# Rotation of K on GpSimd from a ScalarE copy, that of Q left on VectorE, and x2 plus its norm as one affine step of ScalarE

## What is computed

```python
x = x + L0_attn(layernorm(x))                      # stage A
u = layernorm(x)                                   # stage B from here
q = xpos(u @ Wq, inverse_scale=False)              # x * cos + rot * sin
k = xpos(ctx_1024 @ Wk, inverse_scale=True)
v = ctx_1024 @ Wv
x = x + (q @ k^T * decay_mask) @ v                 # x2
y = layernorm(x)
x = x + (y + moe_top2(rms_norm(y)))                # 8 experts, the FFN has its own skip
```

## Time and profile before

| | us |
|---|---|
| median of 3 runs | 457.16 (456.96 to 457.54) |
| the profiled execution, its own time | 458.88 |
| its span, first to last instruction | 457.1 |
| PE, DVE, ACT, POOL busy | 380.0, 275.5, 258.8, 199.6 |
| granted TensorE clock, mean | 0.931 of full |

### The profile page before, as it was taken

The page is one execution under the profiler, slowest core; times in us unless marked ns, Lnnn a source line. Parts: engine busy times, 40 slices in busy tenths (PEclk is TensorE's granted clock), DMA queues, the critical chain, the costliest instruction groups (busy, mean ns, idle before and its releaser), DMA issues.

```text
span 457.1 us, 10128 instructions
## 1 busy us (share of the span) xinstructions
PE 380.0 (83%) x2600; PEld 272.5 (60%) x2601; DVE 275.5 (60%) x688; ACT 258.8 (57%) x473; POOL 199.6 (44%) x186
## 2 busy tenths in 40 slices
PE   1899997899885211499999999999999999999980
PEld 0687786787774211256666666666666666666650
DVE  3789787979797999554444444454444444444440
ACT  2799786776775631555445545554555555554530
POOL 2634637668788403224343334343443344333221
PEclk9999998999998555599999999999999999999996
DMA  7999850622221240112222222222222322223220
GB/s 248 408 426 403 288 184 1 204 73 70 69 93 62 77 142 1 36 29 45 48 36 36 45 47 35 44 39 47 43 37 37 47 47 35 36 45 45 26 25 11
DMA packets 24645, 41.93 MB, mean 92 GB/s; under 512 B 5040, under 2 KB 20400, under 8 KB 23600
## 3 DMA queue, kind: packets, MB, share of 16 engines
q1 hardware_dynamic: 17088, 31.17, 19.1%
q0 software_dynamic: 7536, 10.52, 14.3%
HBM read 32.17 MB, written 9.50 MB: 91 GB/s over the span
## 4 chain that ended last, share of the span: by engine, by line
PE 67%; DVE 13%; ACT 8%; issue 5%; POOL 2%; DMA 2%; SPq 1%; ACTq 0%; DVEq 0%; POOLq 0%
PE bank L1220 30%; PE bank L1241 6%; PE bank L1270 5%; PE bank L1271 5%; PE bank L1272 5%; ACT arena L434 4%; DVE expert_w L842 3%; PE bank L1107 2%; PE bank L1155 2%; PE bank L1252 2%; DVE expert_w L833 2%; ACT arena L449 2%; PE bank L1164 2%; PE bank L1060 1%; DVE arena L988 1%
## 5 line engine op out<-in xcount | busy, mean ns | idle before, releaser
L1220 PE MATMUL bank<-expert_w,arena 128*128 x702 | 159.2, 364 | 4.4 <-ACT arena L617 4.4
L732 POOL DMA_INDIRECT out<-arena,add_idx x39 | 61.7, 1581 | 114.8 <-ACT arena L598 114.8
L1220 PEld LDWEIGHTS bank<-expert_w,arena 128*128 128x128 f16 x702 | 65.8, 98 | 54.2 <-issue 6.8
L1037 DVE SCALAR_TENSOR_TENSOR arena<-bank,dn_small,arena 128x512 f32<-128x512 f32 x78 | 45.3, 581 | 38.2 <-PE bank L1220 23.4
L722 POOL DMA_INDIRECT arena<-xrow_hbm,take_idx x39 | 38.7, 994 | 58.1 <-PE bank L1252 43.3
L1270 PE MATMUL bank<-expert_w,arena 128*128 x195 | 53.1, 273 | 0.9 <-DVE arena L1021 0.9
L1271 PE MATMUL bank<-expert_w,arena 128*128 x195 | 53.2, 273 | 0.0
L1272 PE MATMUL bank<-expert_w,arena 128*128 x195 | 53.1, 273 | 0.0
L1021 DVE COPY arena<-bank 128x1024 f16<-128x1024 f16 x39 | 27.0, 692 | 37.8 <-PE bank L1241 37.8
L617 ACT ACTIVATE arena<-bank 128x512 f16<-128x512 f16 x39 | 23.3, 597 | 37.1 <-PE bank L1252 37.1
L1043 DVE TENSOR_TENSOR arena<-arena 128x512 f16<-128x512 f32 x39 | 27.0, 692 | 27.1 <-ACT arena L623 27.1
(11 more groups left out here) (179 smaller groups left out, 736.5 us busy)
## 6 DMA issues: line engine op xcount, KB each, us to landing
expert_w<-in_wup SPq DMA_DIRECT2D x8, 1408.0 KB, 17.2
expert_w<-in_wdn SPq DMA_DIRECT2D x10, 640.0 KB, 4.7
rows<-in_x SPq DMA_DIRECT2D x8, 256.0 KB, 6.3
arena<-in_ctxT SPq DMA_DIRECT2D x8, 256.0 KB, 3.2
xrow_hbm<-front SPq DMA_DIRECT2D x8, 256.0 KB, 2.2
out<-rows SPq DMA_DIRECT2D x8, 256.0 KB, 2.7
expert_w<-in_wdn SPq DMA_DIRECT2D x20, 64.0 KB, 4.9
cst_b<-in_consts_b SPq DMA_DIRECT2D x1, 960.0 KB, 13.6
```

The lines of the kernel that those rows point to most:

```text
L732: pool.indirect_dma_start(out=out, in_=yt[:, i % 2], in_offset=None, out_offset=bass.IndirectOffsetOnAxis(ap=add_idx[:, i:i + 1], axis=0), ...
L1037: V.scalar_tensor_tensor(out=hh[:, cols], in0=src, scalar=h_scale[:, ds(e, 1)], in1=sg[:, cols], op0=ALU.mult, op1=ALU.mult).then_inc(s_h, 1)
L1220: last = T.matmul(bank[q][:, 0:n], xsT[:, slot, (2 * a + c) * P:(2 * a + c + 1) * P], up_w[:, ds(w0 + c * UPC + w * 2 * H + lo, n)], start ...
```

## The change

On the K half, ScalarE copies PSUM bank 2 into the SBUF tile `kc` (it takes the place of `sk`) as soon as K is ready. GpSimd then does everything from that copy: the cosine product, the two sine products, a wait for its own products (`s_krot`), and the addition. VectorE keeps the products of Q only, and the addition for Q stays on GpSimd, now behind the four instructions for K.

For x2 plus its norm, GpSimd adds 1 to the reciprocal root, and ScalarE computes row * (1 + r) + bias in place in one pair of instructions, late in its step, behind the transposed copy and the high part of xn. The ScalarE pair in front of u2 and the GpSimd addition L690 are gone.

```diff
 # ScalarE, step_b
-                if live(r, 3, NBATCH):
-                    act.wait_ge(s_r34, b + 1)
-                    if r >= 4:
-                        act.wait_ge(s_x2s, b)
-                    for j in range(2):
-                        last = nc.scalar.activation(sk[:, j], rows[:, ds(b * 2 + j, 1), :].squeeze(1), ACT.Identity,
-                                                    bias=nb3[:, slot, j:j + 1], scale=r34[:, slot, 0, j:j + 1])
-                    last.then_inc(s_s, 1)
...
                 if live(r, 1, NBATCH):
                     b, _, slot = at(it, k, 1)
+                    act.wait_ge(s_K, b + 1)
+                    if r >= 2:
+                        act.wait_ge(s_kr, b)
+                    nc.scalar.activation(kc, bank[2][:, :].rearrange("p (m n) -> p m n", m=2), ACT.Copy).then_inc(s_rk, 1)
                     act.wait_ge(s_V, b + 1)
...
                     if r < NBATCH + 2:
                         xn_high(b)
+                    act.wait_ge(s_r34, b + 1)
+                    act.wait_ge(s_xn, b + 1)
+                    for j in range(2):
+                        row = rows[:, ds(b * 2 + j, 1), :].squeeze(1)
+                        last = nc.scalar.activation(row, row, ACT.Identity, bias=nb3[:, slot, j:j + 1],
+                                                    scale=ve3[:, slot, 0, j:j + 1])
+                    last.then_inc(s_x2s, 1)
 # GpSimd, step_b
-                    for n, (bank_read, rotated, dst) in enumerate(((s_rk, s_kr, kr), (s_rq, s_qr, qr))):
-                        pool.wait_ge(bank_read, b + 1)
-                        if n and r >= 3:
-                            pool.wait_ge(s_xn, b - 1)
-                        nc.gpsimd.tensor_tensor(dst[:, slot], dst[:, slot], rot[:, n], ALU.add).then_inc(rotated, 1)
+                    pool.wait_ge(s_rk, b + 1)
...
+                    nc.gpsimd.tensor_tensor(kr[:, slot], kc, const("kcos").unsqueeze(1).broadcast_to([P, 2, SEQ]), ALU.mult)
+                    for m in range(2):
+                        last = nc.gpsimd.tensor_tensor(rot[:, 0, m], kc[:, 1 - m], const("ksin")[:, m * SEQ:(m + 1) * SEQ], ALU.mult)
+                    last.then_inc(s_krot, 1)
+                    pool.wait_ge(s_krot, b + 1)
+                    nc.gpsimd.tensor_tensor(kr[:, slot], kr[:, slot], rot[:, 0], ALU.add).then_inc(s_kr, 1)
+                    pool.wait_ge(s_rq, b + 1)
+                    if r >= 3:
+                        pool.wait_ge(s_xn, b - 1)
+                    nc.gpsimd.tensor_tensor(qr[:, slot], qr[:, slot], rot[:, 1], ALU.add).then_inc(s_qr, 1)
...
-                    pool.wait_ge(s_s, b + 1)
-                    pool.wait_ge(s_xn, b + 1)
-                    nc.gpsimd.tensor_tensor(rows[:, ds(b * 2, 2), :], sk, rows[:, ds(b * 2, 2), :], ALU.add).then_inc(s_x2s, 1)
...
+                    nc.gpsimd.tensor_tensor(ve3[:, slot, 0], r34[:, slot, 0], const("ones")[:, 0:2], ALU.add)
 # VectorE, step_b
-                    for n, (ready, rotated, read, used, dst, cos, sin) in enumerate((
-                            (s_K, s_kr, s_rk, s_R, kr, const("kcos"), const("ksin")),
-                            (s_Q, s_qr, s_rq, s_R, qr, const("qcos"), const("qsin")))):
...
+                    V.tensor_tensor(qr[:, slot], src, const("qcos").unsqueeze(1).broadcast_to([P, 2, SEQ]), ALU.mult)
+                    for m in range(2):
+                        last = V.tensor_tensor(rot[:, 1, m], src[:, 1 - m], const("qsin")[:, m * SEQ:(m + 1) * SEQ], ALU.mult)
+                    last.then_inc(s_rq, 1)
```

More of the change, by code:

```diff
@@ L177, in build @@
         xn = view(arena, 4480, 2, D)
-        sk = view(arena, 4992, 2, D)
+        kc = view(arena, 4992, 2, SEQ)
         xnT = view(arena, 5504, 2, SEQ)
@@ L255, in build @@
         s_rk, s_rq = sem("k_bank_read"), sem("q_bank_read")
-        s_kr, s_qr = sem("k_rotated"), sem("q_rotated")
+        s_kr, s_qr, s_krot = sem("k_rotated"), sem("q_rotated"), sem("k_products_ready")
         s_vt = sem("v_copied")
@@ L261, in build @@
         s_pp = sem("pool_step")
-        s_s, s_x2s, s_out0 = sem("skip_ready"), sem("x2_plus_skip_ready"), sem("skip_stored")
+        s_x2s, s_out0 = sem("x2_plus_skip_ready"), sem("skip_stored")
         s_xh, s_xl, s_xn = sem("xn_high_ready"), sem("xn_low_ready"), sem("xn_ready")
@@ L554, in step_b @@
                 if live(r, 3, NBATCH):
-                    b, _, _ = at(it, k, 3)
+                    b, _, slot = at(it, k, 3)
                     act.wait_ge(s_tr3, b + 1)
@@ L679, in step_b @@
                     b, _, slot = at(it, k, 1)
[L680 to L684 removed]
+                    pool.wait_ge(s_rk, b + 1)
+                    if r == 1:
+                        pool.wait_ge(s_cstb, 16)
+                    if r >= 3:
+                        pool.wait_ge(s_R, b - 1)
+                    if r >= 2:
+                        pool.wait_ge(s_kr, b)
+                    nc.gpsimd.tensor_tensor(kr[:, slot], kc, const("kcos").unsqueeze(1).broadcast_to([P, 2, SEQ]), ALU.mult)
[5 more added lines that the diff above has]
+                    pool.wait_ge(s_rq, b + 1)
+                    if r >= 3:
+                        pool.wait_ge(s_xn, b - 1)
+                    nc.gpsimd.tensor_tensor(qr[:, slot], qr[:, slot], rot[:, 1], ALU.add).then_inc(s_qr, 1)
                 if live(r, 3, NBATCH):
                     b, _, _ = at(it, k, 3)
[L688 to L690 removed]
                     pool.wait_ge(s_xh, b + 1)
@@ L858, in step_b @@
                     b, _, slot = at(it, k, 1)
-                    for n, (ready, rotated, read, used, dst, cos, sin) in enumerate((
-                            (s_K, s_kr, s_rk, s_R, kr, const("kcos"), const("ksin")),
-                            (s_Q, s_qr, s_rq, s_R, qr, const("qcos"), const("qsin")))):
-                        src = bank[2 + n][:, :].rearrange("p (m n) -> p m n", m=2)
-                        dve.wait_ge(ready, b + 1)
-                        if r >= 2:
-                            dve.wait_ge(rotated, b)
-                        if r >= 3:
-                            dve.wait_ge(used, b - 1)
-                        V.tensor_tensor(dst[:, slot], src, cos.unsqueeze(1).broadcast_to([P, 2, SEQ]), ALU.mult)
-                        for m in range(2):
-                            last = V.tensor_tensor(rot[:, n, m], src[:, 1 - m], sin[:, m * SEQ:(m + 1) * SEQ], ALU.mult)
-                        last.then_inc(read, 1)
+                    src = bank[3][:, :].rearrange("p (m n) -> p m n", m=2)
+                    dve.wait_ge(s_Q, b + 1)
+                    if r >= 2:
+                        dve.wait_ge(s_qr, b)
+                    if r >= 3:
+                        dve.wait_ge(s_R, b - 1)
+                    V.tensor_tensor(qr[:, slot], src, const("qcos").unsqueeze(1).broadcast_to([P, 2, SEQ]), ALU.mult)
+                    for m in range(2):
+                        last = V.tensor_tensor(rot[:, 1, m], src[:, 1 - m], const("qsin")[:, m * SEQ:(m + 1) * SEQ], ALU.mult)
+                    last.then_inc(s_rq, 1)
                 if r == 1:
```

1 line of the change is left out of this document (removed).

## The result

The changed kernel takes **469.55 us** in the median of four runs (467.39 to 471.46), against 457.35 us (456.96 to 457.54) for the kernel before in the same session. The ratio is 1.0267, with a 95% interval of 1.0210 to 1.0323. The change costs 12.2 us. The forecast was 468.2 us, in a range of 460.5 to 474.5. A ratio is estimated from the single runs, so it need not be the quotient of the two medians.

A forecast was written before the change was run, and what follows sets the result against it. Steps 5 to 8 were held by GpSimd's addition for Q, delayed by VectorE's low part: 4 x 13.4 us for 43.4 (+10.2), early steps +0, drain +0.8, sum +11.0; 458.88 becomes 469.9, median 468.2 us, range 460.5 to 474.5.

The forecast's parts named there:

- The mechanism: Stage B: VectorE's low part (L833) delays GpSimd's addition for Q, which holds the scores; full-clock step 11.8 us instead of 10.75.
- The chain for K: Stage B: ScalarE's copy, then GpSimd's products and addition, end at S + 9.0 instead of S + 6.9 (S: start of scores).
- xn held: VectorE, stage B: xn (L890) was to run unhindered, from S + 7.2 to S + 7.9, S being the start of scores.
- The clock: TensorE, steps 5 to 8: gaps near 2 us lower the clock, adding 1.7 us to K; step 13.4 us.
- the state keeps itself up: TensorE, stage B: at the low clock the gap is again 1.9 us, so the low clock recurs in each step.
- The high clock: Rival: TensorE stays at 2.4 GHz, steps 5 to 8 take 49.0 instead of 43.4 us, total 463.6 us; chance 0.22.
- The second L843: Rival: in steps 5, 7, 8 a second low part precedes Q's addition, +4.8 to +5; chance 0.18, shared with dear sine products.
- The hidden chain: Rival: Q's addition gets the port ahead of the low part, K's chain hides, total 455 us; chance 0.07.
- The drain and the early steps: Last scores to routing chain: +0.8 us (0 to 1.5); start to step 5's scores: +0, 1.5 us either way.
- Stage E: After stage B and the serial VectorE chain: nothing edited, so it keeps its length of before.
- From the span to the median: Profiled execution forecast at 469.9 us; before's profiled execution is 1.7 above its median, so the median becomes 468.2 us.

The follow-up runs named there:

- the filler: Changed kernel plus four unread constant products on TensorE at the end of steps 3 to 8: 465.25 us, 1.0188 against the kernel before.
- the addition for Q was freed: Changed kernel without the wait of GpSimd's addition for Q on xn: 472.43 us, 1.0304; the same edit in the kernel before: 458.24 us, 1.0015.

## Why the prediction was right, and where it was off

The direction, the place of the loss and its mechanism were right. That the number came within 1.4 us is in part luck: stage B was 0.7 us and stage E 1.9 us shorter than forecast, and the step from one execution to the median was 3.9 us the other way.

**The mechanism: right.** The scores of steps 5 to 9 start 0.1 us after the addition for Q (0.3 in step 6), 12.3 to 15.0 us apart, and that addition takes 2.58 us beside the low part and ends 1.14 us after it (1.13 was expected). The end of stage B moved by 10.3 us, against 11.0. That the low part beside the chain makes the K part dear is shown by moving it: 9 of the 12 us go, while the same move in before gives nothing. In the steps themselves half of the loss goes; what is left lies in the steps with ScalarE's late copy (5 and 7) and with the low clock (8).

**The chain for K: right to 0.3 us.** K ready at S + 4.2, both sine products in 1.41 us (1.46), addition done at S + 9.3 (9.0). The products started 0.47 us behind the end of ScalarE's copy (112.12), for GpSimd's own roots ran until 112.31 and 0.28 us passed behind them. The prediction let the products start when the copy ends.

**xn held: a step that failed.** The prediction gave L890 the 0.73 us of the earlier trace rows, and the rule that it cites says that an instruction with one input from SBUF doesn't contend. L897 is the same instruction; beside K's sine products and addition it takes 2.21 us. In the rows of before GpSimd was idle when it ran (122.16 to 123.32). The Trainium skill ("SBUF — State Buffer", "Who interferes with whom") exempts single-input instructions only outside the two-port modes, which a `tensor_scalar` can enter: the prediction left this condition out. The trace agrees with the full rule, by the 2.21 us for 0.73. The error is small here, since L843 would have waited for the addition for K in any case, and it moves the full-clock step from 11.8 to 12.3 us together with the late start of the products.

**The clock: right in kind, too large.** The prediction added 1.7 us for the low clock to each of the four steps, 6.8 us. In the trace it fell in two of the four, for 1.3 and 2.7 us; the filler gave back 3.9 us there, and 3.6 us by the ratios. Two gaps that look alike did not end alike: after 2.47 us the scores ran at 1.2 GHz from their first product (2.05 us for 1.10), after 2.27 and 1.84 us they and all behind them ran at 2.4 GHz, and after 2.12 us the scores were fast and the router and K that followed were slow (3.76 us for 1.97). The gap behind each step was as expected, but "the state keeps itself up" was wrong. The prediction took one gap of before (1.92 us) for the only one, and read past a second, 2.31 us ahead of step 3's transposes, which had the low clock behind it too (1.11 us for 0.66); in the trace of before with the low part moved, gaps of 2.31 and 2.09 us in the same places had none. The two errors cancelled: a step took 12.3 us and on average 1.0 for the clock (13.25), where the prediction had 11.8 and 1.6 (13.4).

**The rivals.** The high clock gave 49.0 us for the four steps; with the filler they took 49.1. The sum is a good account of the chain alone, in part by luck: the rival had the steps at 11.8, 12.0, 13.2 and 12.0 us, and they took 12.0, 12.4, 12.5 and 12.2. And the clock did not stay high in after itself. The second L843 did not get in ahead of the addition for Q: in step 7 it starts at 133.75, while that addition has been running since 131.85. The hidden chain failed at the point named for it, the port; with the low part out of the way a one-chunk step is 10.7 us, as in before.

**The drain and the early steps: right.** +0.26 us for a forecast of +0.8, and +0.41 for 0 with 1.5 either way. The expected 1.09 us delay of L503 by the affine doesn't show in the sum.

**Stage E: wrong, by 2 us the other way.** It was to stay as it was. From TensorE's first product of stage E to the end it takes 267.8 us in before and 265.9 in after, and this is no accident of one execution: all seven profiled kernels that rotate K on VectorE take 267.8 to 269.0, and all seven that rotate it on GpSimd 265.4 to 266.6. VectorE's waits from 230 to 440 us differ in one line (L1026 of before is L1033 of after), before first:

```profile
DVE arena L1026 <- issue: 12.7, 31, 0.7
```

```profile
DVE arena L1033 <- issue: 11.0, 32, 0.4
```

No instruction of stage E was edited. In every second tile VectorE comes to this instruction 0.1 us earlier, and the tile is as much shorter. "Issue" means that nothing in the profile explains the wait. What the seven share against the other seven is the K part: three products and their waits less in each body of VectorE's earlier loop, and more instructions on GpSimd and ScalarE there. Why that should matter to stage E was not tested, and stays open.

**From the span to the median.** The profiled pair differs by 8.5 us, the medians by 12.2. The execution of before that was profiled lay 1.5 us above its median and that of after 2.2 us below its own. The prediction allowed for the first (1.7). The second can't be foreseen: after spreads over 467.39 to 471.46 us in its four runs. Before spread over only 0.58 us in the four runs beside it, but over 455.12 to 459.56 us in the runs beside the experiments. The runs at 471 have a mean clock of 0.915 and 0.916, those at 467 and 468 have 0.923 and 0.924, so more low-clock steps are the likely reason; only one of the four has a trace. In sum: for the profiled execution the forecast had 469.9 and it took 467.4, 0.7 us less by stage B and 1.9 by stage E; from there to the median the forecast took 1.7 off, and 2.2 came on. Hence 469.55 against 468.2.

## What to carry to other kernels

VectorE's products with an input from PSUM took no longer beside GpSimd (0.69 us either way), so moving them to GpSimd is only a gain if GpSimd's chain isn't in the path and no two-input work of VectorE lies beside it. Price such a move as a loop over both engines: time that GpSimd gains can return as a hold on VectorE, then on its statistics and roots, then on GpSimd's own next step, as it did when the addition for Q was freed. Before an engine is relieved, look at whether it waits anyway (VectorE waited 1.9 us or more for Q in each of steps 5 to 8 of after), and place the colliding instruction into that wait: here that gave back 2.1%, at least as much as leaving the sine products out altogether (1.6%, with intervals that overlap).

## What the chip showed that had not been expected

- A gap of TensorE of about 2 us or more sometimes lowers the clock and sometimes doesn't, and when it does, the fall may come only about 1 us after work has begun again. Gaps in the trace of after: 2.47 and 1.89 us (low at once), 2.12 and 1.99 us (low from the second group of the scores on), 2.27 and 1.84 us (not low). With the low parts behind the statistics 3.17 us didn't lower it, with the low parts ahead of Q 2.65 us didn't and 2.53 us did. The cost of one fall in steps 5 to 8 of after was 1.3 and 2.7 us.
- GpSimd's hold reaches a VectorE instruction with one input from SBUF: L897, 2.21 us for 0.73. The two engines also hold each other's tiny instructions: GpSimd's root of four elements took 2.40 us for 1.02 beside the low part, and VectorE's two-element instruction of the statistics 0.84 us for 0.17 (low parts ahead of Q).
- Two products of 128x256 on GpSimd take 1.41 us, one of 128x512 takes 1.27. A power of 4 elements takes 1.02 us, one of 16 elements 2.90, longer than two additions of 512.
- Stage E became 1.9 us shorter with no instruction of it changed.
